# A fused block of attention and feed-forward on one core: the lower part of the attention context left in PSUM by TensorE and copied out by ScalarE

## The reference

```
h   = x @ W.T + b + 2 * (x @ A[ids]) @ B[ids]          # linear layer with an adapter per sequence
q   = h @ ((qw_q - 8) * scales_q)   # 32 heads of 128; k and v: 8 heads, each shared by 4 query heads
q,k = rope(q), rope(k)
ctx = softmax(causal(q @ k.T / sqrt(128))) @ v          # 32 heads
x   = x + ctx @ ((qw_o - 8) * scales_o)                 # scales change every 128 input rows
x   = x + ffn(lowrank(x))                               # layer norm, two fake-quantized layers, gelu
```

## Time and profile before

| | |
|---|---|
| median of three runs | 569.2 us (568.51 to 569.67) |
| the profiled execution, its own time | 571.88 us |
| its span, first to last instruction | 569.9 us |
| busy in the span: TensorE, VectorE, GpSimd, ScalarE | 536.8, 498.9, 396.3, 368.7 us |
| granted TensorE clock, mean | 0.996 |

### The profile page before, as it was taken

How to read it: one execution, slowest core, us unless ns; L and a number is a source line. 1 busy time by engine, 2 the same in 40 slices (tenths; PEclk the granted TensorE clock), 3 DMA queues, 4 the chain that set the end, 5 groups by cost and what they waited for, 6 DMA issues and landing times.

```text
span 569.9 us, 10645 instructions
## 1 busy us (share of the span) xinstructions
PE 536.8 (94%) x3190; PEld 322.9 (57%) x3190; DVE 498.9 (88%) x651; ACT 368.7 (65%) x941; POOL 396.3 (70%) x410
## 2 busy tenths in 40 slices
PE   8898989999999999999999999999999999987885
PEld 6543456556655665566556655665566556653432
DVE  4765967998999899989998999899989998986897
ACT  3365567667666766676667665766576656665895
POOL 3004488699769976997699769976997699852063
PEclk9989999999999999999999999999999999999999
DMA  8842244512451245124512451245124312300003
GB/s 302 181 108 74 65 121 139 131 47 60 135 132 46 60 134 132 43 60 134 131 43 60 134 131 43 60 134 131 43 63 134 93 42 61 85 4 2 0 20 129
DMA packets 38172, 51.93 MB, mean 91 GB/s; under 512 B 12100, under 2 KB 20452, under 8 KB 38148
## 3 DMA queue, kind: packets, MB, share of 16 engines
q1 hardware_dynamic: 35652, 46.94, 31.0%
q10 hardware_dynamic: 2016, 3.48, 1.9%
q0 software_dynamic: 480, 1.22, 0.6%
HBM read 28.55 MB, written 2.10 MB: 54 GB/s over the span
## 4 chain that ended last, share of the span: by engine, by line
PE 56%; DVE 21%; issue 7%; ACT 6%; SPq 4%; POOL 3%; DMA 2%; DVEq 0%; ACTq 0%; POOLq 0%
PE pair L1528 16%; PE pair L1529 16%; PE flow L1652 8%; PE flow L1517 6%; DVE accT L1215 4%; PE flow L1644 4%; DVE raw_q L1201 2%; DVE ctx_lo L1222 2%; SPq L408 2%; DVE raw_k L1201 2%; ACT probs L753 2%; DVE y_max L1311 2%; DVE raw_v L1201 1%; PE flow L1435 1%; PE flow L1522 1%
## 5 line engine op out<-in xcount | busy, mean ns | idle before, releaser
L1215 DVE SCALAR_TENSOR_TENSOR accT<-pair,so_now,accT 128x1024 f32<-128x1024 f32 x125 | 156.4, 1272 | 11.8 <-PE pair L1529 11.2
L1201 DVE SCALAR_TENSOR_TENSOR raw_q<-pair,sc_now,raw_q 128x1024 f32<-128x1024 f32 x90 | 115.5, 1283 | 6.2 <-ACT raw_q L809 2.8
L589 POOL TENSOR_TENSOR probs<-probs,rowinv 128x512 f32<-128x512 f32 x64 | 66.6, 1041 | 65.6 <-DVE rowinv L1188 65.2
L753 ACT ACTIVATE probs<-flow,negmax 128x128 f32<-128x128 f32 x248 | 87.5, 367 | 36.4 <-DVE negmax L1169 36.4
L1528 PE MATMUL pair<-ctx_hi,wo 128*128 128x512 f16 x256 | 97.2, 380 | 5.0 <-issue 2.0
L1529 PE MATMUL pair<-ctx_lo,wo 128*128 128x512 f16 x256 | 97.0, 379 | 0.0
L1528 PE MATMUL pair<-h_hi,wq 128*128 128x512 f16 x240 | 91.3, 380 | 1.1 <-DVE accT L1215 1.1
L1529 PE MATMUL pair<-h_lo,wq 128*128 128x512 f16 x240 | 91.0, 379 | 0.0
L558 POOL TENSOR_TENSOR rope_s<-swap_q,consts 128x512 f32<-128x512 f32 x62 | 78.9, 1272 | 10.2 <-DMA swap_q<-raw_q 10.2
L832 ACT ACTIVATE ctx_hi<-flow,ctx_gain 128x512 f16<-128x512 f32 x64 | 44.0, 687 | 60.8 <-PE flow L1652 60.3
L570 POOL TENSOR_TENSOR qT<-rope_c,rope_s 128x512 f32<-128x512 f32 x62 | 78.9, 1273 | 4.4
(11 more groups left out here) (278 smaller groups left out, 904.9 us busy)
## 6 DMA issues: line engine op xcount, KB each, us to landing
swap_q<-raw_q SPq DMA_DIRECT2D x62, 256.0 KB, 3.7
wq_i<-in_L_attn_qw_q SPq DMA_DIRECT2D x8, 1024.0 KB, 5.6
wo_i<-in_L_attn_qw_o SPq DMA_DIRECT2D x32, 256.0 KB, 2.7
swap_k<-raw_k SPq DMA_DIRECT2D x14, 256.0 KB, 3.6
wkv_i<-in_L_attn_qw_k SPq DMA_DIRECT2D x8, 256.0 KB, 3.6
wkv_i<-in_L_attn_qw_v SPq DMA_DIRECT2D x8, 256.0 KB, 4.0
stage<-in_x ACTq DMA_DIRECT2D x4, 256.0 KB, 4.6
probs<-in_L_ffn_w ACTq DMA_DIRECT2D x4, 256.0 KB, 8.1
```

Of the source, the lines that this page charges most:

```text
L589: pool.tensor_tensor(pr, pr, rowinv[:, f, :].unsqueeze(2).broadcast_to([P, HB, P]), ALU.mult).then_inc(probs_done, 1)
L753: e = act.activation(probs[:, 0, f, seq(b)], bank[:, seq(b)], ACT.Exp, bias=negmax[:, f, b:b + 1], accum_out=rowsum[:, f, b:b + 1])
L1201: dve.scalar_tensor_tensor(out=into, in0=flat(pair[pair_of(h, (kind, j), last, first)][:, :, :]), scalar=sc_now[:, scale_slot(kind, h), j: ...
L1215: dve.scalar_tensor_tensor(out=a, in0=flat(pair[pair_of(h, (O, c), last, first)][:, :, :]), scalar=so_now[:, (h if c == 0 else h - 1) % 2, ...
```

## The change

Six of the eight halves of a group (`LEFT_BY_PE`: both halves of heads 1, 2 and 3, in all groups but the last) get their lower part in another way. After ScalarE has copied the bank to `ctx_hi`, TensorE multiplies `ctx_hi` by minus the identity (`minus_h`, f16) and adds it on top of the context in the same bank, which leaves exactly the rest; ScalarE then copies the bank to `ctx_lo`. VectorE has no part in it there. For this the gain is applied earlier: `v_now` is multiplied by `ctx_gain` when it is copied, and the context comes out scaled, so `ctx_hi` is a plain copy and the remaining `split_context` (head 0, and the last group) a plain subtraction. The semaphore `ctx_split` becomes two, one per half.

Around that, orders are changed: in head 3, (V, 3) goes ahead of (Q, 3) on TensorE and on VectorE; ScalarE copies the second lower part between the two masks (head 3: ahead of `keep_values`). In the opening, TensorE runs `lora_rows` ahead of its wait for `peaks_made` and the transpose of the peaks; VectorE takes the adapters' peaks (which wait for a DMA) after two `clip_weights` and `keep_scales` instead of ahead of them; ScalarE runs `take_weights(4)` after the first four `keep_upper` instead of ahead of `keep_weights(2)`.

```diff
-                  [(Q, 0), (O, 1), (Q, 1), (Q, 2), (Q, 3), (V, 3), (O, 2), (O, 3), (O, 0)]]
+                  [(Q, 0), (O, 1), (Q, 1), (Q, 2), (V, 3), (Q, 3), (O, 2), (O, 3), (O, 0)]]
+        LEFT_BY_PE = [(1, 0), (1, 1), (2, 0), (2, 1), (3, 0), (3, 1)]
...
             keep_weights(0)
             round_weights(5)
-            take_weights(4)
             keep_weights(2)
             act.wait_ge(gain_made, 1)
             for k in range(C):
                 keep_upper(k)
+            take_weights(4)
...
+                    def keep_lower_context(f):
+                        if not left_by_pe(h, f, last):
+                            return
+                        act.wait_ge(ctx_left, lefts_by(g, h, f))
+                        act.activation(ctx_lo[:, h % 2, half[f]], flow[f][:, :], ACT.Copy).then_inc(ctx_split[f], 1)
...
+                    keep_lower_context(0)
                     keep_upper_context(1)
...
+                        seed_mask(0)
+                        keep_lower_context(1)
+                        if h == 3:
+                            keep_values(g + 1, 0)
                     seed_mask(1)
...
             find_scales(2)
-            peaks_of_adapters()
             clip_weights(2)
             keep_scales()
             clip_weights(3)
+            peaks_of_adapters()
...
                     def split_context(f):
+                        if left_by_pe(h, f, last):
+                            return
                         dve.wait_ge(ctx_kept, 2 * n + f + 1)
-                        dve.scalar_tensor_tensor(out=ctx_lo[:, h % 2, half[f]], in0=flow[f][:, :], scalar=ctx_gain[:, 0:1],
-                                                 in1=ctx_hi[:, h % 2, half[f]], op0=ALU.mult, op1=ALU.subtract).then_inc(ctx_split, 1)
+                        dve.tensor_tensor(ctx_lo[:, h % 2, half[f]], flow[f][:, :], ctx_hi[:, h % 2, half[f]],
+                                          ALU.subtract).then_inc(ctx_split[f], 1)
...
             pe.wait_ge(d_la, 16 * 2 * B)
+            lora_rows()
             pe.wait_ge(peaks_made, 1)
             pe.transpose(banks[5][0:N_PEAKS, 0:P], peaks[:, :], ident).then_inc(peaks_turned, 1)
-            lora_rows()
...
+                    def leave_lower(f):
+                        if not left_by_pe(h, f, last):
+                            return
+                        pe.wait_ge(ctx_kept, 2 * n + f + 1)
+                        pe.matmul(flow[f][:, :], minus_h[:, :], ctx_hi[:, h % 2, half[f]], start=False, stop=True,
+                                  skip_group_check=True).then_inc(ctx_left, 1)
...
                     if h == 3:
-                        project(V, 3)
+                        project(Q, 3)
+                    leave_lower(0)
                     context(1)
                     if not (last and h >= 2):
                         output(2)
+                    leave_lower(1)
                     values_ahead(0)
```

More of the change, by code:

```diff
@@ L84, in build @@
         ident_h = sb("ident_h", [P, P], F16)
+        minus_h = sb("minus_h", [P, P], F16)
         tri_b = sb("tri_b", [P, P], BF16)
@@ L219, in build @@
         probsT_done, probsT_kept = sem("probsT_done"), sem("probsT_kept")
-        pv_done, ctx_kept, ctx_split = sem("pv_done"), sem("ctx_kept"), sem("ctx_split")
+        pv_done, ctx_kept, ctx_left = sem("pv_done"), sem("ctx_kept"), sem("ctx_left")
+        ctx_split = [sem("ctx0_split"), sem("ctx1_split")]
         mask_seeded = sem("mask_seeded")
@@ L340, in seeded, with left_by_pe, lefts_by @@
             return h < SEEDED and not (last and h >= 2)
+        LEFT_BY_PE = [(1, 0), (1, 1), (2, 0), (2, 1), (3, 0), (3, 1)]
+        def left_by_pe(h, f, last):
+            return (h, f) in LEFT_BY_PE and not last
+        def lefts_by(g, h, f):
+            return len(LEFT_BY_PE) * g + LEFT_BY_PE.index((h, f)) + 1
         def score_bank(f, last_head):
@@ L799, in _ @@
                 act.wait_ge(vT_done, f + 1)
-                act.activation(v_now[:, HB * f:HB * f + HB, :], per_seq(banks[4 + f]), ACT.Copy).then_inc(v_kept, 1)
+                act.activation(v_now[:, HB * f:HB * f + HB, :], per_seq(banks[4 + f]), ACT.Copy,
+                               scale=ctx_gain[:, 0:1]).then_inc(v_kept, 1)
             def body(g, first, last):
@@ L819, in keep_values @@
                         act.wait_ge(vT_done, 2 * turned + f + 1)
-                        act.activation(v_now[:, HB * f:HB * f + HB, :], per_seq(flow[f][:, :]), ACT.Copy).then_inc(v_kept, 1)
+                        act.activation(v_now[:, HB * f:HB * f + HB, :], per_seq(flow[f][:, :]), ACT.Copy,
+                                       scale=ctx_gain[:, 0:1]).then_inc(v_kept, 1)
                     def seed_mask(f):
@@ L825, in seed_mask @@
                             return
-                        act.wait_ge(ctx_split, 2 * n + f + 1)
+                        act.wait_ge(ctx_split[f], n + 1)
                         act.activation(per_seq(flow[f][:, :]), on_each_seq(tri), ACT.Copy).then_inc(mask_seeded, 1)
@@ L831, in keep_upper_context @@
                         act.wait_ge(pv_done, 2 * n + f + 1)
-                        act.activation(ctx_hi[:, h % 2, half[f]], flow[f][:, :], ACT.Copy,
-                                       scale=ctx_gain[:, 0:1]).then_inc(ctx_kept, 1)
+                        act.activation(ctx_hi[:, h % 2, half[f]], flow[f][:, :], ACT.Copy).then_inc(ctx_kept, 1)
+                    def keep_lower_context(f):
[3 more added lines that the diff above has]
+                        act.activation(ctx_lo[:, h % 2, half[f]], flow[f][:, :], ACT.Copy).then_inc(ctx_split[f], 1)
                     def drain_query():
@@ L873, in body @@
                         drain_first(V, g + 1)
+                    keep_lower_context(0)
                     keep_upper_context(1)
-                    if h == 3 and not last:
-                        keep_values(g + 1, 0)
-                    if not (first and h == 0):
+                    if not left_by_pe(h, 1, last):
+                        if h == 3 and not last:
+                            keep_values(g + 1, 0)
+                        if not (first and h == 0):
+                            seed_mask(0)
+                    else:
                         seed_mask(0)
+                        keep_lower_context(1)
+                        if h == 3:
+                            keep_values(g + 1, 0)
                     seed_mask(1)
@@ L983, in _ @@
             dve.wait_ge(d_const, 16)
+            dve.tensor_scalar(minus_h[:, :], ident, -1.0, None, ALU.mult)
             dve.tensor_copy(ident_b[:, :], ident).then_inc(consts_made, 1)
@@ L1232, in body @@
                     for j in range(1, C):
-                        drain(Q, j)
+                        drain(*((V, 3) if h == 3 and j == 3 else (Q, j)))
                         if first and h == 0 and j == 1:
@@ L1241, in body @@
                     if h == 3:
-                        drain(V, 3)
+                        drain(Q, 3)
                     split_context(1)
@@ L1633, in output @@
                             pe.wait_ge(wo_made, n + 1)
-                            pe.wait_ge(ctx_split, 2 * n + 2)
+                            for f in range(2):
+                                pe.wait_ge(ctx_split[f], n + 1)
                         free_pair(O, c)
@@ L1641, in turn_probs @@
                         if last and h == 3:
-                            pe.wait_ge(ctx_split, 2 * (n - 1) + f + 1)
+                            pe.wait_ge(ctx_split[f], n)
                         for b in range(HB):
@@ L1660, in values_ahead @@
                                 pe.wait_ge(dve_drained, drains_by(g, h, (V, 3), first, last))
-                            pe.wait_ge(ctx_split, 2 * n + f + 1)
+                            pe.wait_ge(ctx_split[f], n + 1)
                             turn_values(f, flow[f])
@@ L1683, in body @@
                         turn_probs(0)
-                    project(Q, 3)
+                    project(*((V, 3) if h == 3 else (Q, 3)))
                     if last and h >= 2:
```

## The result

The changed kernel takes 561.91 us at the median of 4 runs (559.83 to 562.61), the kernel before, run beside it, 569.43 (4 runs); the ratio is 0.9855, 95% interval 0.9833 to 0.9877. It is 7.5 us faster, and 1.6 us above the 560.3 on record, inside the range. The sum came out nearly right.

A forecast was written before the change was run, and what follows sets the result against it. TensorE was taken to bound most of a group, with VectorE ending most remaining waits. Groups -4.9 and opening -4.0 took the profiled 571.88 to 563.0 us, and the median, 2.7 under it, to 560.3; range 555 to 566.

The forecast's parts named there:

- The groups, -4.9 on record: Seven changed groups, each forecast 0.7 us shorter: -4.9 us in all.
- (V, 3) ahead of (Q, 3): Head 3: V's drain ends some 1.9 us earlier, so TensorE's 0.73 us stall ahead of the turned values goes: -0.73 a group.
- +1.30: TensorE, each group: six added f16 matmuls of 128x512 at 0.22 us cost 1.30 us.
- -0.44: Heads 1 and 3: the first half's `leave_lower(0)` runs inside TensorE's stall for `probsT`, hiding 0.22 us in each.
- -0.61: Start of head 2: VectorE's drains come about 1.0 us earlier, so TensorE's stalls of 0.30 and 0.31 vanish.
- -0.45: Heads 2 and 3: GpSimd's product and `probsT` come earlier, saving TensorE 0.45 us a group of small waits.
- +0.40: Copies moved to ScalarE: head 3's scores wait 0.25 us for `v_now`, plus 0.05 for each of three handoffs.
- The opening, -4.0 on record: Before the groups: reordering lets `h_scaled` start near 34.0 and `linear(6)` at 45.6 instead of 49.63, saving 4.0 us.
- (A): Opening gains only its first part, 1.3 us, since rounding or a load then ends last: 563.0 us; chance 0.12.
- (B): Groups: TensorE is the bound and VectorE's relief is worth nothing, +0.97 us a group: 572.0 us; chance 0.05.
- (C): Groups: each new matmul stalls 0.38 us for `ctx_hi`, 2.3 us a group, making it slower, 576 us; chance 0.04.
- (D): Groups: more gain than could be followed, 1.4 us a group: 555.4 us; chance 0.13.

The follow-up runs named there:

- gain_in_v: Kernel before with only the context's gain moved from `ctx_hi` and VectorE's split to `v_now`; 566.9 us (1 run), period 56.75.
- twice: Changed kernel with a second matmul, of zero weights, beside each `leave_lower`, six more a group; 571.0 us (1 run), period 57.29.
- v3_first: Kernel before with only (V, 3) put ahead of (Q, 3) in head 3; 569.9 us, ratio 0.9988, period 56.91.
- q3_first: Changed kernel with (Q, 3) put ahead of (V, 3) again in head 3; 563.8 us, ratio 0.9894, period 56.09.
- left_all: Changed kernel with all eight halves' lower parts left by TensorE, head 0 too; 569.0 us, ratio 0.9968, period 56.59.
- dve_pad: Changed kernel with a dummy 128x512 f32 multiplication on VectorE at each of the six places of a split; 583.6 us (1 run), period 58.57.

## Why the prediction was right, and where it was not

**The groups, -4.9 on record, -6.2 in the trace.** The period was to be 56.3 (56.1 to 56.7) and is 56.08, just below the range. Term by term:

- *(V, 3) ahead of (Q, 3), -0.73: this step failed.* Alone it gives 0.08, on top of the rest 0.01. The stall was the end of a full queue: VectorE was late there because it was late everywhere. Moving one drain forward left its work as it was, and the wait went to GpSimd's K and to the steps behind. What took the stall away is the relief, which I had credited with head 2's stalls and the small ones only.
- *The relief and its price, +1.30 - 0.44 - 0.61 - 0.45 + 0.40 = +0.20: it measured -0.66.* The 0.73 belongs here, which would make -0.53; the other 0.13 is spread over its parts. Of its parts, -0.61 is right: both stalls of the earlier trace rows at head 2's start are gone. -0.44 is right against the kernel before: in the earlier trace rows the last matmul ahead of `context(1)` starts at 353.28, and the trace has the matmul behind that context at 354.62, 1.34 later; after the change it is 346.57 to 347.89, 1.32, with `leave_lower(0)` in between. Against `gain_in_v` it is a little less: there the same stretch is 1.25 (349.00 to 350.25), so 0.07 of the matmul's 0.22 is paid. `twice` shows the limit: a second matmul there is not hidden. +0.40 was too much by more than half: against `gain_in_v` the wait for `v_now` grew by 0.05 (0.25 was on record for it), the context of head 0's first half starts 0.10 later behind its step than there, and no `leave_lower` waits for `ctx_hi`. A bound failed in its arithmetic too: 0.1 for each of twelve handoffs is 1.2 a group, not the 0.5 on record.
- *The gain's operand, 0 on record, -0.23 measured.* I had noted that `ctx_hi` loses it and priced only the new copies by it. The Trainium skill (ScalarE: Activation LUTs, What ACT_TABLE_LOAD costs) gives about 93 ns per pointer operand; `ctx_hi` fell by 90 (687 to 597) and `v_now` rose by 90 (597 to 687 in `gain_in_v`). The rule and the trace agree; I applied it to one instruction and not to the one that stands between a context and its lower half.
- The measured parts are -0.23 - 0.66 - 0.01 = -0.90, from 56.98 to 56.08. They are steps of one chain of kernels and add up by construction. By another chain (exchange, operand, lower parts) the same -0.90 is -0.07 - 0.35 - 0.48, so how much belongs to which part depends on the order. That the sum on record, -0.53 and then -0.7 by hand, came near -0.90 is in part luck: the exchange was put 0.72 too high, the relief and the operand together 1.09 too low.

**The opening, -4.0 on record.** It was 3.2 to 3.3 in the profile and 0.6 to 1.4 as a median of runs. Two of the steps came nearly as written, as two timeline rows of ScalarE show beside the earlier trace rows:

```profile
33.34 2.78 ACT L716 ACTIVATE h_scaled<-pair,bias_gained,gain 128x512 f32<-128x512 f32 x4 [2.22 <-PE pair L1478]
...
42.13 0.69 ACT L754 ACTIVATE raw_k<-pair,sc_now 128x512 f32<-128x512 f32 x1 [1.35 <-PE pair L1539]
```

`h_scaled` was to start at 34.0 and the drain at 41.9, and with it `linear(6)` at 45.6; it starts at 45.87. The same execution had the clock at 0.62 and 0.52 from 32 to 36 us, on `linear(4)`, where before it fell on `lora_rows`. The term was mis-sized by what the sum had no term for, the granted clock. The profiled execution of before was at the long end of its kernel's runs (span 569.9, where the 40 later ones have a median near 568.4), and I made the sum against it. Its 2.93 us for `lora_rows` were taken at the lower clock: `v3_first`, with the same order, shows the same 32 matmuls in 1.93:

```profile
27.49 1.93 PE L1398 MATMUL pair<-accT,qT 128*32 128x256 f32 x32
```

So part of the four microseconds was a loss of that one execution and not of its order.

**Together.** The groups give 5.9 (5.2 for six periods and 0.7 for the first group) to 6.2 (seven times 0.89), and the opening 0.6 to 1.4 by the medians, 6.5 to 7.6 together. The measured 7.5 lies in that, near its end. On record were -4.9 and -4.0. The two errors, a group too little by 0.2 and an opening too much, nearly cancelled, and that is luck.

**The rivals.** (A), only the opening's first part, was close in size (-1.3) and wrong in cause: rounding and loads did not end last. (B), TensorE as the bound, is refuted by `q3_first` and true of the kernel after: its stalls are 1.1 us of 56.08, and `twice` pays nearly in full. I had read the Trainium skill (Perfetto Trace Analysis, Identifying the Most-Contended Engine) as speaking against a load on TensorE. That was a misreading: the page does not take TensorE's matmul busy time for this, but its MFU or the share of its weight loads. The latter is 57%, against VectorE's 88%, and by it VectorE is the engine to relieve, as the change does. Yet the share is only 59% in the changed kernel, where the starts leave TensorE 1.1 us of stalls in 56.08. How full TensorE was is told here by the starts alone: three matmuls were well placed there and eight too many. (C) did not occur in the changed kernel and did in `left_all`. (D) asked for 1.4 a group. Both forecasts of busy time were too large. VectorE's busy time fell by 24.8 us, not 31: a split of 745 ns overlaps its neighbour (start to start 0.67), and a group lost 3.6 (52.98 to 49.41), 0.6 for each of six. ScalarE's rose by 19.3, not 25, mostly because its 64 copies to `ctx_hi` became 90 ns shorter, 5.8 us.

## What to carry to other kernels

A stall at the end of a full queue is a symptom. Before moving the late instruction ahead, ask what the engine was doing for the ten microseconds ahead of it. Try the relief of that engine alone and the move alone, since their gains don't add. Shift work onto the busiest engine only as far as there are stalls to hide it in (here three matmuls gave as much as six, and eight gave half of it back), and look at what stands in the queue of the engine that must answer. When one profiled execution is the base of a sum for a short serial stretch, put the spread of executions and the granted clock of that stretch beside it. The period of a loop, by contrast, repeats to a few hundredths.

## What the runs showed of the hardware

- TensorE's granted clock fell to its lower level for a few microseconds (by the windows, each fall lost as much work as 1.7 us at full speed does), at different places in different executions of the same order. In `q3_first`:

```profile
76.00:78.00 2.00, 0.10 (x1) 0.13 (x2) 1.44 (x3) 1.75 (x7) 0.96 (x1) 1.00 0.37 131
78.00:80.00 2.00, 2.00 (x11) 2.00 (x12) 1.43 (x2) 0.33 (x1) 2.00 (x3) 0.56 0.00 0
80.00:82.00 2.00, 2.00 (x9) 1.08 (x8) 0.69 (x1) 1.37 (x3) 1.86 (x3) 0.58 0.15 35
```

  TensorE (the second number) had been idle for nearly 2 us. The clock (third from the end) then stood between its two levels for two stretches, that is part of the time at 1.2 and part at 2.4 GHz. In the changed kernel's profile it fell at 32 us behind a stretch in which TensorE had been busy 1.54 of 2.00, and in five of the fourteen profiles it did not fall in the first 110 us.
- A multiplication of 128x512 f32 from and to SBUF on VectorE took between 681 and 1816 ns beside GpSimd's own products, and GpSimd's busy time in a group rose from 46.75 to 49.21 with six of them. In one group of `dve_pad` six pads took 0.68 to 1.80 us; GpSimd's product beside one of the short ones (0.68, at 345.90) took 1.80, where the same product took 1.27 on the mean in the kernel before. The subtraction that reads PSUM took 679 to 693 ns in the same run.
